# A convolution chain with second-order attention: transpositions in place of products, a padded half tile, and a new order of the steps without y

## The reference, cut to what matters

```python
# layer 0: rotate, clip, quantise to 8 bits over all samples, rotate back
im = relu(x) as (256, 32*3136);  mn = mean(im, 1);  im = im - mn
p = clip(u.T @ im, -cv, cv);  dmax, dmin = p.max(1), p.min(1)
q = round((p - dmin) * 255 / (dmax - dmin)) ...   # back to the scale of p
x1 = u @ q - mean(u @ q) + mn

# layer 1: attention over channels from a covariance, per sample
h = relu(bn(w_conv1 @ x1))            # 256 channels
d = relu(bn(w_dr @ h + b_dr))         # 128 channels
cov = (d - mean d) @ (d - mean d).T / M          # 128 x 128
r = einsum('cjh,bch->bcj', w_row, bn(cov));  r = r + b_row       # 512 values
att = sigmoid(w_fc @ r + b_fc)
out = x1 * att
```

## Time and profile before

| | |
|---|---|
| median of 3 runs | 1867.75 us |
| the profiled execution | 1868.28 us |
| its span | 1866.5 us |
| busy: TensorE | 91% |
| VectorE, ScalarE, GpSimd | 84%, 79%, 25% |
| mean granted TensorE clock | 0.954 |

### The profile page before, as it was taken

How to read it: one execution, slowest core, us unless ns; L and a number is a source line. 1 busy time by engine, 2 the same in 40 slices (tenths; PEclk the granted TensorE clock), 3 DMA queues, 4 the chain that set the end, 5 groups by cost and what they waited for, 6 DMA issues and landing times.

```text
span 1866.5 us, 40162 instructions
## 1 busy us (share of the span) xinstructions
PE 1695.2 (91%) x13394; PEld 1317.1 (71%) x13394; DVE 1576.0 (84%) x2897; ACT 1475.6 (79%) x2244; POOL 460.2 (25%) x136
## 2 busy tenths in 40 slices
PE   8999999999993235588899999999999999999999
PEld 8999999999992011366566666666666766666665
DVE  6888888888887788689988888888888888888886
ACT  7777777777778997788778878788788787888886
POOL 7888888888880000000000000000000000000000
PEclk9999999999996567699999999999999999999999
DMA  9998998998999999405546546455465464554535
GB/s 333 375 375 305 375 370 305 378 365 313 373 353 388 430 430 429 194 2 201 191 156 235 169 167 227 157 201 193 165 221 175 163 233 162 189 204 166 213 139 208
DMA packets 141135, 477.37 MB, mean 256 GB/s; under 512 B 10656, under 2 KB 33568, under 8 KB 126368
## 3 DMA queue, kind: packets, MB, share of 16 engines
q1 hardware_dynamic: 141088, 476.75, 69.2%
HBM read 284.04 MB, written 192.68 MB: 255 GB/s over the span
## 4 chain that ended last, share of the span: by engine, by line
PE 51%; DVE 4%; ACT 0%; issue 0%; DVEq 0%; ACTq 0%
PE y_ps L1014 16%; PE z_ps L1040 16%; PE d_ps L965 13%; PE cov_ps L947 5%; DVE hl L1181 1%; DVE gg L1203 1%; PE ch_ps L1025 1%; DVE g L1193 0%; DVE p_res L1274 0%; DVE qr L1149 0%; PE ch_ps L978 0%; PE ch_ps L977 0%; DVE q L1156 0%; PE y_ps L994 0%; PE cov_ps L950 0%
## 5 line engine op out<-in xcount | busy, mean ns | idle before, releaser
L299 POOL TENSOR_TENSOR xl<-early,xh 128x1568 fp32r<-128x1568 f32 x128 | 459.3, 3589 | 97.1 <-ACT xh L258 97.1
L1040 PE MATMUL z_ps<-qr,wl 128*128 128x512 f16 (+2 forms) x896 | 314.5, 354 | 0.0
L1040 PE MATMUL z_ps<-qr,wh 128*128 128x512 f16 (+2 forms) x896 | 314.2, 354 | 0.0
L1181 DVE TENSOR_TENSOR hl<-h,hh 128x1024 f16<-128x1024 f32 (+2 forms) x224 | 243.9, 1089 | 74.5 <-ACT hh L1097 74.3
L258 ACT ACTIVATE xh<-early 128x1568 fp32r<-128x1568 f32 x128 | 194.1, 1517 | 139.8 <-PE pp L316 139.7
L965 PE MATMUL d_ps<-vh,hh 128*128 128x128 f16 x1600 | 280.1, 219 | 7.5 <-DVE hl L1181 7.5
L1092 ACT ACTIVATE h<-z_ps,sb_h 128x512 f32<-128x512 f32 (+2 forms) x448 | 264.0, 625 | 23.6 <-PE z_ps L1040 20.5
L965 PE MATMUL d_ps<-vl,hh 128*128 128x128 f16 x1600 | 279.9, 219 | 0.0
L965 PE MATMUL d_ps<-vh,hl 128*128 128x128 f16 x1600 | 279.9, 219 | 0.0
L316 PE MATMUL pp<-xh,uh 128*128 128x392 f32 x1024 | 267.4, 342 | 9.1 <-ACT xh L258 9.1
L1014 PE MATMUL y_ps<-qr,udh 128*128 128x512 f16 (+2 forms) x784 | 274.1, 353 | 0.0
(11 more groups left out here) (198 smaller groups left out, 2999.7 us busy)
## 6 DMA issues: line engine op xcount, KB each, us to landing
early<-in_x_dram SPq DMA_DIRECT2D x128, 784.0 KB, 6.9
out_dram<-p_res SPq DMA_DIRECT2D x30, 3136.0 KB, 10.2
early<-p_scratch SPq DMA_DIRECT2D x42, 1568.0 KB, 12.7
p_res<-p_scratch SPq DMA_DIRECT2D x112, 512.0 KB, 4.4
p_scratch<-early SPq DMA_DIRECT2D x56, 784.0 KB, 7.8
p_scratch<-late SPq DMA_DIRECT2D x56, 784.0 KB, 7.8
p_res<-p_scratch SPq DMA_DIRECT2D x56, 384.0 KB, 3.2
late_tile<-p_scratch SPq DMA_DIRECT2D x13, 1568.0 KB, 12.8
```

Of the source, the lines that this page charges most:

```text
L299: nc.gpsimd.tensor_tensor(xl[:, k % 2], xs[:, k], xh[:, k % 2].bitcast(F32), ALU.subtract).then_inc(split_done, 1)
L1040: last = nc.tensor.matmul(z_ps[:, m, 0:w], part[:, k, m * P:(m + 1) * P], qr[:, a, k, columns(s)], start=k == 0 and part is wh, stop=k == ...
L1181: nc.vector.tensor_tensor(hl[:, par, :, 0:w], h32[:, par, :, 0:w], hh[:, par, :, 0:w], ALU.subtract).then_inc(h_split, 1)
```

## The change

The change has these parts.

- **The half tile.** `gg` gets a place G = 4 for the last tile of a sample, whose rows 64 to 127 are zero once and for all. The copy to fp16 and the low half write the two whole tiles with one instruction and the half one with another; the covariance's products always take 128 rows.
- **Transpositions in attention.** The two products of `spread` become two transpositions (the row sums are first written across a tile with `ones` in place of `ident`). `logits` becomes two transpositions of `weighted` and a reduction on VectorE, `logit_sb`. In phases of an existing sample, `logits` runs at the end of step 3 instead of within step 4.
- **Steps without y.** TensorE takes z, then d and the covariance, then `spread` and `logits`. VectorE takes the low half of g first, then the conversion; the sums of the attention come behind `hl`. In steps 1 to 3 ScalarE scales both halves of the y made early.
- **Between the first two stages.** The mean, the early part of maxima and minima, and the shift are taken at the end of the first stage; the small operations work on both ends at once.
- **Into the main stage.** `z_ps` and `y_ps` are allocated in the second stage already; the first two chunks of z are formed at its end (two more places of `halve`), phase 0 alternates between both, and z runs one step ahead there. The constant of y moves to step 4 of phase 0.
- **Alignment.** `p_res`, `early` and `late_tile` start at multiples of 256 bytes.

```diff
-        p_res = sb("p_res", [P, RES, K, M])
+        p_res = sb("p_res", [P, RES, K, M], align=LINE)
...
+                act.wait_ge(x_summed, 1)
+                nc.scalar.activation(mn[:], mn[:], ACT.Copy, scale=1.0 / (N * M)).then_inc(mean_done, 1)
...
+                pe.wait_ge(mean_done, 1)
+                pe.wait_ge(psum_read, K * (N * SUBS - 1))
+                for m in range(K):
+                    for k in range(K):
+                        last = nc.tensor.matmul(shift[:, m:m + 1], u_sb[:, k, m * P:(m + 1) * P],
+                                                mn[:, k:k + 1], start=k == 0, stop=k == K - 1)
+                last.then_inc(shift_done, 1)
...
-            (i, t) for i in range(2 * RES + 1, PAIRS - 1) for t in range(3 + (i % 2 == 0))]
+            (i, t) for i in range(2 * RES + 1, PAIRS - 1) for t in range(3 + (i >= PAIRS - 4))]
...
+                for c in range(EARLY_Z):
+                    pe.wait_ge(q_halved, MADE * CH + c + 1)
+                    pe.wait_ge(quantised, TILES * PAIRS - 1 + PARTS if c > 0 else TILES * (PAIRS - 1) + 2)
+                    for m in range(K):
+                        for k in range(K):
+                            for part_of in (wh, wl):
+                                last = nc.tensor.matmul(
+                                    early_z[c][:, m, 0:widths[c]], part_of[:, k, m * P:(m + 1) * P],
+                                    q16[:, (MADE * CH + c) % 2, k, 0:widths[c]],
+                                    start=k == 0 and part_of is wh, stop=k == K - 1 and part_of is wl)
+                        last.then_inc(z_done, 1)
...
+            def g_places(c):
+                whole = widths[c] // P
+                return [(P, slice(0, whole), slice(0, whole))] + (
+                    [(SHORT, slice(whole, whole + 1), slice(G, G + 1))] if c == CH - 1 else [])
...
+            def vector_scales(s):
+
+                return not 1 <= s <= 3
...
-                            q = min(P, widths[c] - t * P)
                             end = c == CH - 1 and t == tiles[c] - 1
-                            nc.tensor.matmul(cov_ps[:, 0:2 * P + 1], gg[0:q, par, t, 0:P],
-                                             gg[0:q, par, t, 0:2 * P + 1], start=c == 0 and t == 0,
+                            place = G if end else t
+                            nc.tensor.matmul(cov_ps[:, 0:2 * P + 1], gg[:, par, place, 0:P],
+                                             gg[:, par, place, 0:2 * P + 1], start=c == 0 and t == 0,
                                              stop=False)
...
-                        nc.tensor.matmul(ch_ps[:, 0:P], hl_sb[:], ident[:], start=True, stop=True)
-                        nc.tensor.matmul(ch_ps[:, P:2 * P], ones[:], dg[:], start=True,
-                                         stop=True).then_inc(spread_done, 1)
+                        nc.tensor.transpose(ch_ps[:, 0:P], hl_sb[:], ident[:])
+                        nc.tensor.transpose(ch_ps[:, P:2 * P], dg[:], ident[:]).then_inc(spread_done, 1)
...
-                    if s == Y_LAG and exists(r2, a, back=1):
+                    if s == (3 if exists(r2, a) else Y_LAG) and exists(r2, a, back=1):
                         pe.wait_ge(weighted_done, J * n)
+
+                        wait_from(pe, logits_summed, n - 1)
                         for m in range(K):
-                            last = nc.tensor.matmul(ch_ps[:, 2 * P + m:2 * P + m + 1], weighted[:, m],
-                                                    ones[:, 0:1], start=True, stop=True)
+                            last = nc.tensor.transpose(ch_ps[:, (2 + m) * P:(3 + m) * P], weighted[:, m], ident[:])
                         last.then_inc(logits_done, 1)
...
+                        if first_phase(r2, a):
+                            if s == 4:
+                                constant_of_y()
+                            if EARLY_Z <= s + 1 < CH:
+                                wide(r2, a, s + 1)
+                        elif exists(r2, a):
+                            wide(r2, a, s)
+                        if has_no_y(r2, a, s):
+                            if s == 1:
+                                covariance(r2, a, s)
+                            reduced(r2, a, s)
+                            if s != 1:
+                                covariance(r2, a, s)
+                            spread(r2, a, s)
+                            logits(r2, a, s)
+                            continue
...
                         reduced(r2, a, s)
                         if s != 1:
                             covariance(r2, a, s)
+                        if exists(r2, a):
+                            logits(r2, a, s)
...
-                            act.wait_ge(logits_done, n)
+                            act.wait_ge(logits_summed, n)
...
+                    if s == Y_LAG and exists(r2, a, back=1):
+                        dve.wait_ge(logits_done, n)
+
+                        wait_from(dve, att_done, n - 1)
+                        nc.vector.tensor_reduce(logit_sb[:], ch_ps[:, 2 * P:].rearrange("p (m c) -> p m c", m=K), AX_X,
+                                                ALU.add).then_inc(logits_summed, 1)
...
-                        if s == 1:
+                        if s == 1 or has_no_y(r2, a, s):
                             low_half_of_g(r2, a, s)
...
+                        if not has_no_y(r2, a, s):
+                            sums_of_covariance(r2, a, s)
                         if has_no_y(r2, a, s):
                             rectified_g(r2, a, s)
                             low_half_of_h(r2, a, s)
-                            if has(r2, a, s, CH + Y_LAG):
+                            sums_of_covariance(r2, a, s)
+                            if has(r2, a, s, CH + Y_LAG) and vector_scales(s):
```

More of the change, by code:

```diff
@@ L174, in layer_kernel @@
             pp = ps("pp", [P, 2, K, 2, BANK], a)
+            shift = pp[:, 0, 0, 0, BANK - K:BANK]
+            assert SC <= BANK - K
             block = a.enter_context(nc.Block())
@@ L416, in layer_kernel @@
             scaled_u = u_sb
[L417 to L421, removed]
+            shift_ps = z_ps[:, 0]
+            spread_ps = z_ps[:, 1]
+            sum_w, plain_bh, sum_v, sum_u = (shift_ps[:, n * K:(n + 1) * K] for n in range(4))
+            u_ps = y_ps[:, 0].rearrange("p (k c) -> p k c", k=K)
+            w1_ps = y_ps[:, 1].rearrange("p (k c) -> p k c", k=K)
             w1u_ps = ps("w1u_ps", [P, K, C], b)
@@ L457, in _ @@
                 last.then_inc(turned, 1)
[L458 to L463, removed]
                 for j in range(J):
@@ L1083, in phase @@
                             wait_from(act, cov_done, g - 3)
-                            nc.scalar.activation(gg[0:dq, (CH * a + s) % 2, 0:dt, 0:P], g32[0:dq, 0:dt],
-                                                 ACT.Copy).then_inc(gh_done, 1)
+                            for rows, source, place in g_places((s - 2) % CH):
+                                last = nc.scalar.activation(gg[0:rows, (CH * a + s) % 2, place, 0:P],
+                                                            g32[0:rows, source], ACT.Copy)
+                            last.then_inc(gh_done, 1)
                         if exists(r2, a):
@@ L1126, in phase @@
                             if made(o):
-                                kept = kept_y(o, c)[:, 0]
-                                nc.scalar.activation(kept, kept, ACT.Identity, scale=att_cy[:, 0, 0:1],
-                                                     bias=att_cy[:, 0, 1:2]).then_inc(y_free, K)
+                                own = 1 if vector_scales(s) else K
+                                for m in range(own):
+                                    kept = kept_y(o, c)[:, m]
+                                    last = nc.scalar.activation(kept, kept, ACT.Identity, scale=att_cy[:, m, 0:1],
+                                                                bias=att_cy[:, m, 1:2])
+                                last.then_inc(y_free, K)
                                 continue
@@ L1202, in low_half_of_g @@
                         dve.wait_ge(gh_done, g - 1)
-                        nc.vector.tensor_tensor(gg[0:dq, par, 0:dt, P:2 * P], g32[0:dq, 0:dt],
-                                                gg[0:dq, par, 0:dt, 0:P], ALU.subtract).then_inc(g_split, 1)
+                        for rows, source, place in g_places((s - 2) % CH):
+                            last = nc.vector.tensor_tensor(gg[0:rows, par, place, P:2 * P], g32[0:rows, source],
+                                                           gg[0:rows, par, place, 0:P], ALU.subtract)
```

256 lines of the change are left out of this document (146 added, 110 removed).

## The result

The changed kernel takes **1896.77 us** (median of five runs, 1893.65 to 1897.88) against 1868.95 for the kernel before beside it: a ratio of 1.0148, interval 1.0137 to 1.0160, 27.8 us slower. The prediction had 1880 us and a range from 1868 to 1891. Its direction was right; its size was not, and the result lies outside the range.

A forecast was written before the change was run, and what follows sets the result against it. It took TensorE as leading VectorE in phases with y, VectorE as pacing those without, and DMA as bounding quantising. +7.8 + 9.3 - 2.7 - 2.0 = +12.4 us on 1868.28 gave 1880 us, range 1868 to 1891.

The forecast's parts named there:

- The deciding edit: Logits at the end of step 3: TensorE would wait 0.87 us for `weighted`, delaying z of step 4.
- The first rival: TensorE stays the bound: phases with y lose 0.77 us each, 27 times, kernel at 1842 us; chance 0.05.
- Phases with y: Phases 5 to 31 of the main stage: +0.29 us each from the logits' wait and later covariance input, +7.8 us in all.
- Phases without y: Phases 1 to 4 of the main stage: 2.8 us for each of 1 to 3, 0.9 for 4, +9.3 us.
- The walk: One phase without y, summed by trace durations: 19.7 us from `hl` of step 0 to step 4 (+1.3), then +1.5.
- Start of quantising: From `mn` to the first quantised tile, 4.70 us shrink to 2.0 with statistics moved earlier: -2.7 us.
- Start of the main stage: ScalarE waits only for the bias, not the first z: -2.0 us, taken between 0 and -4.
- Half tile: Padding saves 0.17 us of TensorE per phase, but the covariance's input comes 0.19 us later.
- the rival that aligned loads pay 11: The DMA-bound 180 us gets 6% faster, giving 11 us back: no change, 1869 us; chance 0.06.
- The scalings' relief: Phases without y: three of seven scalings leave VectorE, 1.3 us per phase.
- Only the phases with y wait: Rival: relief and delay cancel in phases without y, so +7.8 - 4.7 = +3, 1871 us; chance 0.14.
- Transpositions are no cheaper than products: Rival: 0.34 us more in each cycle, 31 times, 1891 us; chance 0.07.

The follow-up runs named there:

- run 1: Changed kernel with the logits' two transpositions ahead of the reducing products of step 4 again, in all phases: 1872.72 us, ratio 1.0023.
- run 2: Changed kernel with the logits ahead of the reducing products of step 4 in the phases with y only: 1886.82 us, ratio 1.0094.
- run 3: Changed kernel with the logits ahead of the reducing products of step 4 in phases 1 to 4 only: 1882.95 us, ratio 1.0079.
- run 4: Changed kernel with 13 products of 512 columns, whose result nobody reads, ahead of the logits of phases 1 to 4: 1886.38 us, ratio 1.0097.
- Run 5: On top of run 1, steps without y have VectorE's covariance sums ahead of rectified g and no separate TensorE order: 1861.58 us, ratio 0.9969.
- run 6: On top of run 5, the logits are two products with ones again, without the reduction; spread stays transposed: 1857.14 us, ratio 0.9944.
- run 7: Run 6 with the half tile as before the change (products of 64 rows, one copy, one subtraction): 1856.98 us, ratio 0.9944.
- run 10: Run 6 with tile buffers aligned to 32 bytes as in the kernel before: 1859.03 us, ratio 0.9946.
- run 11: Run 6 with all seven scalings of a phase without y on VectorE again: 1860.54 us, ratio 0.9955.
- runs 1 and 12: Run 1 has its own line; the other is run 6 with spread as two fp32 products again: 1859.44 us, ratio 0.9949.
- run 9: Run 6 with the second early z waiting for the same quantised tile as the first: 1855.94 us, ratio 0.9929.
- run 8: Changed kernel with the second early z waiting for the same quantised tile as the first: 1895.13 us, ratio 1.0146.

## Why the prediction was right in direction and wrong in size

**The deciding edit was the right one.** "TensorE is in order, so z of step 4 stands behind the wait for `weighted`": runs 1 to 3 put 23 of the 28 us on that place alone. The first rival (TensorE stays the bound, 1842 us) is refuted by the wait itself, and also in run 2, where the place is restored and the 27 phases are only 1.1 us under those of before.

**Phases with y: +7.8 forecast, +9.5 measured.** The wait was forecast at 0.87 us and is 0.54 to 0.58. The net per phase was forecast at +0.29 and is +0.35. In the middle phases the period is 34.46 against 34.06. The terms: transpositions start 0.11 us apart at the full clock, where I had taken 0.055 by halving the spacing of the earlier trace rows. That was a misreading: I took the clock there for the low one, and the row of that stretch in the kernel before has it at 1.00.

```profile
564.68:565.50 0.82, 0.82 (x8) 0.82 (x9) 0.77 (x3) 0.00 (x0) 0.00 (x0) 1.00 0.36 153
```

So `spread` saved 0.23 and not 0.34, and the logits 0.09 to 0.15 and not 0.26. These errors are partly cancelled by the shorter wait, so that the period with y came out close partly by luck. The Trainium skill's page "TensorE: Matmul & The Clock Gate", section "PE-mode transpose", gives about 275 ns in a kernel's context for a 128x128 tile (in bf16); the trace has, in fp32, 0.27 as the duration of one and 0.11 as the distance to the next, and only the distance enters a sum.

**Phases without y: +9.3 forecast, +18.3 measured. This is the step that failed**: "I walked one phase with the durations of these rows". The walk itself held. From `hl` of step 0 to `hl` of step 4 it gave 19.7 us, and from there to the next phase's 9.91 + 1.5 = 11.4. In run 4, where TensorE is kept busy, these stretches of phase 2 are 19.68 us (833.43 to 853.11) and 11.76, and all four intervals are 8.8 us longer than before. In the changed kernel they are 21.34 us (836.20 to 857.54) and 12.93. The difference, 1.7 and 1.2 us, is the clock, one low stretch in each of the two: the durations of the walk were those of a TensorE at the full clock, and behind the wait for `weighted`, which the walk takes for granted without giving it a length (3.32 us here), it falls. What was missing is the question what a wait does to the engine that waits. The price is 142.09 - 132.60 = 9.5 us. The Trainium skill's page "TensorE: Matmul & The Clock Gate", section "HAM oscillation", describes a kernel in which TensorE waits for a DMA in every turn of a loop and the products behind each wait run at the low clock. The granted clock of 0.90 in phase 2 agrees, for a wait for VectorE, though here the first 0.9 us behind the wait were still at the full level. This was the rule to weigh against the change.

**Start of quantising: -2.7 forecast, -2.9 measured** (569.39 to 566.49 for the first quantised tile); profiles of the other runs have 565.96 to 568.04 for it.

**Start of the main stage: -2.0 forecast, and -1.1 in all at the first `weighted`.** ScalarE's first h came 1.9 us earlier (775.30 against 777.18) and the first d 4.1 (779.50 against 783.58), so the starts paid. The gain was lost between the first d and the first `weighted`, because phase 1's steps 1 to 3 have no y either, and I had counted the new order only from there on. Run 5, with the old order, has 811.90: -5.1 us against before, near the forecast of -4.7. This is a second step that failed, worth 3.6 us in the forecast: the new order was priced at nothing ahead of the first `weighted`, and there it costs 3.9 us (815.82 to 811.90).

**Tail: 0 forecast, +1.9 measured.** Of the last attention I had not counted the reduction on its way. Without it (run 6) the tail is 15.0 us again.

**Half tile, alignment, scalings.** The half tile's saving and its cost cancel over the cycle as a whole (run 7); I had counted the saving as lost in the wait and the later input as 0.19 us a phase. The alignment's 0 held as far as can be told, within 2 to 3 us (run 10), which refutes the rival that aligned loads pay 11. The scalings' relief was 0.8 us a phase (run 11).

**The rivals.** "Only the phases with y wait" is refuted by 18.3 us. "Transpositions are no cheaper than products" gave 1891, and 1894 with the 275 ns of the Trainium skill as a spacing, nearest to the measured time, but for a wrong reason: runs 1 and 12 show them at half the price.

What the change holds of use is in run 9: earlier statistics and early z, three scalings on ScalarE, `spread` transposed, with the logits at step 4 as products and the sums in the old order. The earlier statistics and the early z were not undone one by one, so their share is read from the profiles alone.

## What to carry to other kernels

A walk that finds a new idle stretch on TensorE isn't finished there: look in the trace for what the granted clock does behind idle stretches of that length, in more than one place, and price what follows at both levels; an experiment with products that nobody reads tells the clock's part from the wait's. Move work to an earlier place on an in-order engine only if its input is ready there, since all that stands behind it waits too. And cheaper instructions pay only where the engine holds the period: here 0.53 us saved per phase came back as waits elsewhere.

## What the runs showed that was not expected

- Filling idle time of TensorE with useless products made the kernel 9.5 us faster. In phase 2, 2.97 us of them bought 2.85 (34.28 to 31.43).
- After a wait of 3.32 us TensorE still did its first 0.9 us at the full clock, and the low level came then, for about 3.3 us (853.1 to 856.4), and once more from 863.2 to 866.6. A wait of 0.58 us did nothing to the clock; one of 2.00 was followed by the low level in run 1 and not in run 3, one of 2.30 in the changed kernel and not in run 4. Whoever looks at the clock only where the wait is does not see it.
- In run 9 the second early z ran right behind the first and took 1.89 us for eight products of 512 columns. In the changed kernel, where TensorE is idle for 2.78 us between the two, it takes 3.56 (768.50 to 772.06). In run 9 the clock rose while the last products of the first z ran (at about 766.2), and the second z followed without a gap.
- A transposition of 128x128 in fp32 starts 0.11 us after the one before it at the full clock and 0.21 at the low one. The transpositions of the earlier trace rows ran at the full one in the kernel before (565.04 and 565.15) and at the low one in run 8, where the same tiles come so:

```profile
566.02 0.42 PE L492 MATMUL y_ps<-ident,w_sb 128*128 128x128 f32 x1
566.24 0.42 PE L494 MATMUL y_ps<-ident,u_sb 128*128 128x128 f32 x1
```

```profile
564.90:566.20 1.30, 0.63 (x3) 0.66 (x4) 0.92 (x7) 0.00 (x0) 0.00 (x0) 0.50 0.66 280
```
